# A decoder layer on one NeuronCore: the plan of attention's last quarter drawn up anew, with 42 identity transposes added on TensorE

## What is computed

```
x = x + self_attention(layernorm(x))            # 16 heads of 64, causal
x = x + cross_attention(layernorm(x), ctx, mask) # one head of 256, 64 context rows a batch
x = x + ffn(layernorm(x))
ffn(h): h = silu(h @ w1 * s1) * (h @ w2 * s2)   # 256 -> 1024
        h = gelu(h @ h1 * s);  h = gelu(h @ h2 * s)   # 1024 -> 1024, twice
        return h @ w3 * s                        # 1024 -> 256
```

## Time and profile before

| | |
|---|---|
| median of three runs | 1535.09 us (1532.70, 1535.09, 1535.42) |
| the profiled execution | 1538.07 us, of which its span, first to last instruction, is 1536.3 us |
| busy of the span | PE 98%, PEld 83%, DVE 71%, ACT 62%, POOL 31% |
| mean granted TensorE clock | 0.992 of full speed |

### The profile page before, as it was taken

One profiled execution on the slowest core, in us unless ns is written; L12 is line 12 of the kernel. 1 busy time (PEld: TensorE's weight loads), 2 busy tenths in 40 slices (PEclk: granted clock), 3 DMA queues, 4 the chain that ended last, 5 costly groups with the idle time before them and its releaser, 6 DMA issues.

```text
span 1536.3 us, 29271 instructions
## 1 busy us (share of the span) xinstructions
PE 1506.7 (98%) x10784; PEld 1281.0 (83%) x10784; DVE 1092.3 (71%) x2748; ACT 956.1 (62%) x2246; POOL 482.7 (31%) x763
## 2 busy tenths in 40 slices
PE   8999999999999999999998899999999999999998
PEld 6888888888888888888887788888888888888887
DVE  7999999999999999998999456644553533433432
ACT  5988788888788888888887454445444532222222
POOL 2545454454544445545451001100110211111110
PEclk8999999999999999999999999999999999999999
DMA  4000000000000000000024223421112622222221
GB/s 151 2 1 2 29 2 29 1 2 29 1 29 1 2 29 2 29 1 2 22 90 138 106 79 115 131 103 69 62 70 101 208 88 84 84 83 83 83 84 42
DMA packets 55769, 87.16 MB, mean 57 GB/s; under 512 B 4160, under 2 KB 33216, under 8 KB 55616
## 3 DMA queue, kind: packets, MB, share of 16 engines
q1 hardware_dynamic: 55616, 85.10, 16.4%
HBM read 55.72 MB, written 29.36 MB: 55 GB/s over the span
## 4 chain that ended last, share of the span: by engine, by line
PE 89%; DVE 5%; ACT 2%; DMA 2%; issue 1%; POOL 0%; SPq 0%; DVEq 0%
PE bank L988 14%; PE bank L990 12%; PE bank L634 10%; PE bank L554 9%; PE bank L606 8%; PE bank L556 7%; PE bank L555 7%; PE bank L618 6%; PE bank L996 2%; PE bank L1096 2%; PE bank L1088 2%; PE bank L1089 2%; PE bank L1090 2%; DMA pf<-h_scratch 1%; PE bank L1118 1%; PE bank L1127 1%
## 5 line engine op out<-in xcount | busy, mean ns | idle before, releaser
L820 POOL TENSOR_SCALAR P<-P,stats 128x512 f32<-128x512 f32 (+3 forms) x512 | 267.8, 542 | 362.8 <-DVE stats L798 362.7
L693 ACT ACTIVATE P<-P,stats 128x128 f32<-128x128 f32 (+3 forms) x512 | 283.7, 560 | 19.0 <-DVE stats L790 18.6
L657 ACT ACTIVATE PT<-bank 128x512 fp32r<-128x512 f32 (+1 forms) x384 | 185.7, 524 | 85.2 <-PE bank L618 84.3
L790 DVE CUSTOM_DVE_ANT_0 P<-bank,cmask 128x512 f32<-128x512 f32 (+3 forms) x512 | 228.9, 483 | 3.2 <-PE bank L606 2.4
L707 DVE TENSOR_TENSOR PT<-bank,PT 128x512 fp32r<-128x512 f32 (+1 forms) x384 | 218.6, 594 | 4.9 <-ACT PT L657 3.5
L1267 DVE TENSOR_TENSOR Hb<-gt,Hb 128x512 fp32r<-128x512 f32 x128 | 90.7, 710 | 162.8 <-ACT Hb L1135 162.0
L988 PE MATMUL bank<-w,hw 128*128 128x512 f32 x512 | 200.9, 392 | 4.2 <-DVE w L1267 4.2
L988 PE MATMUL bank<-Hb,hw 128*128 128x512 f32 x512 | 203.1, 397 | 0.0
L634 PEld LDWEIGHTS bank<-PT,V 128*128 128x128 f32 x1024 | 164.3, 189 | 17.1 <-DVE PT L707 0.7
L990 PE MATMUL bank<-Hb,hw 128*128 128x512 f32 x448 | 175.4, 391 | 0.0
L634 PE MATMUL bank<-PT,V 128*128 128x512 f32 (+3 forms) x1024 | 174.7, 318 | 0.0
(11 more groups left out here) (218 smaller groups left out, 3327.2 us busy)
## 6 DMA issues: line engine op xcount, KB each, us to landing
h_scratch<-go SPq DMA_DIRECT2D x64, 256.0 KB, 2.1
xs<-x_scratch SPq DMA_DIRECT2D x23, 512.0 KB, 4.0
qf<-h_scratch SPq DMA_DIRECT2D x32, 256.0 KB, 4.0
pf<-h_scratch SPq DMA_DIRECT2D x32, 256.0 KB, 4.9
stageA<-in_h SPq DMA_DIRECT2D x14, 512.0 KB, 3.8
x_scratch<-x SPq DMA_DIRECT2D x8, 512.0 KB, 3.1
x_scratch<-xs SPq DMA_DIRECT2D x8, 512.0 KB, 3.0
out<-xns SPq DMA_DIRECT2D x16, 256.0 KB, 2.3
```

The source lines that it names most:

```text
L657: return e.activation(dst, src, ACT.Copy, scale=scale)
L693: e.activation(p, p, ACT.Exp, bias=st_[:, k:k + 1], scale=-1.0, accum_out=st_[:, 8 + k:9 + k]).then_inc(s_exp, 1)
L790: e.tensor_tensor_reduce(P_tile(P, i, a), banks["S", P, max(i, 1)][a][:, slice(*S_COLS[i])], cmask[:, 512 - n:512], -1.0, 3.0e38, ALU.add, ...
L820: e.tensor_scalar(p, p, stats[P % 4][:, k:k + 1], 1.0, ALU.mult, ALU.mult).then_inc(s_norm, 1)
```

## The change

The four tables of `TAIL` are replaced (SP's too, by one move). Each engine has the same steps as before, in another order; `HEAD`, `BATCH` and `later()` are untouched. In addition a helper gives TensorE 20 transposes of the identity matrix ahead of `AV.63.0`, and 22 ahead of `xt.0.1.0`, all of them written into the bank that the step has just claimed and then overwrites.

```diff
     "SP": """
-        xload.0 st.6 mb ld.0 ld.1 ld.2 ld.3 ld.6 ld.5 ld.4 ld.7 ld.8 ld.9 ld.10 ld.11 ld.13 st.7 ld.14 ld.12
+        xload.0 st.6 mb ld.0 ld.1 ld.2 ld.3 ld.6 ld.5 ld.4 ld.7 ld.8 ld.9 ld.10 ld.11 ld.13 ld.14 st.7 ld.12
         ld.15 xload.1 ld.16""",
...
+    def keep_warm(e, out, n):
+
+
+        for _ in range(n):
+            e.transpose(out[:, 0:128], ident[:, :], ident[:, :])
+
...
             out, = claim(w, ("AV", P, a))
+            if (P, a) == (NP - 1, 0):
+                keep_warm(e, out, 20)
             w.wait_ge(s_vlo, 4 * (P // 4) + 4)
...
                 out, = claim(w, item)
+                if a == [0, 1, 0]:
+                    keep_warm(e, out, 22)
                 w.wait_ge(s_ln2, ln_at(b, which) + 4)
```

More of the change, by code:

```diff
@@ L115 @@
     "PE": """
[L116 to L125, removed]
@@ L126 @@
-    "ACT": """
[L127 to L148, removed]
@@ L149 @@
-    "DVE": """
[L150 to L174, removed]
@@ L175 @@
[L175 to L185 removed]
+        S.54.2 k.55 v.57 T.53.1 O.52 q.55 S.54.1 T.53.0 k.56 S.55.3 S.55.2 AV.53.0 T.54.2 AV.53.1 T.54.0 S.55.1
@@ new lines @@
+        T.54.1 q.56 k.57 AV.54.0 AV.54.1 O.53 S.56.3 T.55.1 O.54 S.56.2 T.55.2 S.56.1 T.55.0 v.58 v.59 q.57
+        AV.55.0 AV.55.1 S.57.3 T.56.2 T.56.0 v.60 S.57.2 S.57.1 T.56.1 k.58 q.58 AV.56.0 AV.56.1 O.55 T.57.2
+        S.58.3 S.58.2 S.58.1 T.57.0 v.61 T.57.1 k.59 AV.57.0 q.59 AV.57.1 O.56 T.58.2 S.59.3 T.58.0 S.59.2
+        S.59.1 v.62 v.63 k.60 T.58.1 AV.58.0 q.60 AV.58.1 O.57 T.59.2 S.60.3 T.59.0 S.60.2 S.60.1 k.61 T.59.1
+        q.61 AV.59.0 O.58 S.61.3 T.60.2 S.61.2 S.61.1 AV.59.1 k.62 T.60.0 T.60.1 q.62 xt.0.0.0 AV.60.0 AV.60.1
@@ new lines @@
+    "DVE": """
+        ql.54 ys.52.0 lsum.0.0 ys.52.1 vl.56 pl.53.2.0 os.51 r.53.0 m.54.3.0 pl.53.2.1 m.54.2.0 m.54.2.1
+        m.54.3.1 kl.55 lnorm.0.0 pl.53.1.1 os.52 r.54.2 vl.57 pl.53.1.0 m.54.0.1 m.54.1.0 ql.55 m.54.0.0
+        m.54.1.1 pl.53.0.1 pl.53.0.0 kl.56 m.55.2.1 r.54.0 m.55.3.1 m.55.3.0 m.55.2.0 ys.53.0 pl.54.2.0
+        pl.54.2.1 pl.54.0.0 m.55.1.1 m.55.0.0 ys.53.1 m.55.0.1 pl.54.0.1 pl.54.1.0 pl.54.1.1 m.55.1.0 r.55.2
+        ql.56 kl.57 r.55.0 ys.54.0 ys.54.1 os.53 m.56.3.1 m.56.3.0 pl.55.1.0 os.54 pl.55.1.1 m.56.2.0 pl.55.2.1
+        m.56.0.0 m.56.0.1 pl.55.2.0 m.56.2.1 pl.55.0.0 m.56.1.0 pl.55.0.1 r.56.2 m.56.1.1 vl.58 vl.59 ql.57
+        r.56.0 ys.55.0 ys.55.1 m.57.3.0 pl.56.2.0 m.57.3.1 pl.56.0.0 pl.56.2.1 pl.56.0.1 vl.60 m.57.1.1 m.57.0.0
+        m.57.0.1 pl.56.1.0 m.57.2.0 m.57.2.1 pl.56.1.1 m.57.1.0 r.57.2 r.57.0 kl.58 ql.58 ys.56.0 ys.56.1 os.55
+        pl.57.2.1 pl.57.2.0 m.58.3.0 m.58.2.1 m.58.2.0 m.58.0.0 m.58.0.1 m.58.3.1 pl.57.0.1 m.58.1.0 pl.57.0.0
+        m.58.1.1 pl.57.1.1 vl.61 pl.57.1.0 r.58.2 ys.57.0 kl.59 ql.59 r.58.0 ys.57.1 os.56 pl.58.2.1 pl.58.2.0
+        m.59.3.0 m.59.3.1 m.59.2.1 m.59.1.0 m.59.0.1 m.59.0.0 m.59.2.0 pl.58.0.0 pl.58.0.1 vl.62 m.59.1.1 bqa
+        vl.63 kl.60 pl.58.1.1 pl.58.1.0 r.59.2 r.59.0 mask ys.58.0 ql.60 ys.58.1 os.57 pl.59.2.1 pl.59.2.0
+        m.60.3.0 m.60.3.1 pl.59.0.0 m.60.2.0 pl.59.0.1 m.60.1.0 m.60.2.1 m.60.1.1 m.60.0.0 m.60.0.1 kl.61 r.60.2
+        pl.59.1.1 ql.61 pl.59.1.0 r.60.0 os.58 ys.59.0 m.61.3.0 m.61.2.0 m.61.2.1 m.61.1.1 m.61.1.0 m.61.3.1
+        m.61.0.1 m.61.0.0 pl.60.2.1 pl.60.2.0 ys.59.1 kl.62 pl.60.0.1 pl.60.0.0 pl.60.1.0 pl.60.1.1 r.61.2
+        xtl.0.0.0 ql.62 ys.60.0 r.61.0 ys.60.1 xtl.0.0.1 os.59 pl.61.2.1 pl.61.2.0 m.62.3.0 m.62.2.1 m.62.3.1
+        m.62.2.0 fl.0 pl.61.0.0 m.62.0.0 os.60 fl.1 pl.61.1.1 m.62.1.0 pl.61.0.1 kl.63 r.62.2 m.62.1.1 fl.2
+        ql.63 m.62.0.1 ys.61.0 fl.3 xka.0 pl.61.1.0 bql xkl.0 r.62.0 xka.1 fl.4 ys.61.1 xkl.1 pl.62.2.0 m.63.2.0
+        m.63.2.1 m.63.3.1 pl.62.2.1 xva.0 xva.1 m.63.3.0 xfl.0 fl.5 r.63.2 xfl.1 m.63.1.0 pl.62.1.0 m.63.1.1
+        pl.62.0.0 pl.62.1.1 m.63.0.0 pl.62.0.1 m.63.0.1 fl.6 xvl.0 r.63.0 xs1.0 xs2.0 xs3.0 xs4.0 os.61 ys.62.0
+        xvl.1 xr.0 ys.62.1 pl.63.0.0 pl.63.2.1 xpl.0 pl.63.0.1 pl.63.1.0 pl.63.1.1 xoa.0.0 os.62 fl.7 pl.63.2.0
+        xoa.0.1 lsum.0.1 ys.63.0 fl.8 xva.2 ys.63.1 lnorm.0.1 xva.3 flag.2 fl.9 xtl.0.1.0 xtl.0.1.1 fl.10 fm.2
+        fl.11 xvl.2 xvl.3 os.63 os.64 hm.0.0 hm.0.1 hl.0.0 hm.0.2 hl.0.1 hm.0.3 hl.0.2 hl.0.3 hm.0.4 fl.12
+        hl.0.4 hm.0.5 lsum.1.0 flag.3 hl.0.5 fm.3 hm.0.6 hm.0.7 lnorm.1.0 hl.0.6 hl.0.7 fl.13 fl.14 fl.15 fl.16
+        flag.0""",
```

40 lines of the change are left out of this document (36 added, 4 removed).

## The result

The changed kernel takes 1538.18 us (median of 8 runs, 1536.06 to 1541.4), the kernel before 1534.95 us (8 runs). The ratio is 1.0023, 95% interval 1.0014 to 1.0033: 2.2 to 5.1 us slower, by the best value 3.5. The medians themselves are 3.2 us apart.

A forecast was written before the change was run, and what follows sets the result against it. It took TensorE to bound attention from 672 to 788 us and VectorE's queue the end, 788 to 823; 0.45 + 0.7 + 0.0 to 0.1, about +1.1 us, on the median 1535.09 gave 1536.2 us, range 1531.0 to 1539.5.

The forecast's parts named there:

- case A: Whole kernel: the forecast itself, with both new costs, at the 20 transposes and at `xs.1`; 1534 to 1538 us, chance 0.50.
- rival C: Both batches: transposes don't raise the clock, so the 20 take 4.4 us and `ys.63.0` is 4.5 late; 1539.0 us, chance 0.16.
- part 1: Order up to `lnorm.0.1`: VectorE's 2.9 us idle goes, 1.0 us of small operations comes; its end moves from 822.35 to 820.4.
- L: End of `lnorm.0.1`, 822.35 us in the kernel before; forecast 822.8, 0.45 us later.
- part 2: 20 transposes ahead of `AV.63.0`: behind the claim, they begin where the wait ends; `ys.63.0` 1.6 to 3.3 us late, 2.4 taken.
- part 3: 22 transposes ahead of `xt.0.1.0`: they run in TensorE's wait for `lnorm.0.1`, 2.4 us at high clock in 3.5 left; no cost.
- part 4: From `lnorm.0.1`'s end to `xs.1`: a 4.0 us wait replaces the 4.46; resumes 1.2 us earlier, net 0.7 later with low clock.
- part 5: 672 to 788 us: slack at `AV.53.0` turns from 1.6 to -0.4 us; between 0 and 1.6 lost, 0.1 taken.
- I take 1.9: Low clock behind the wait at `xs.1`: 1.9 us lost, from 2.1 and 1.7 lost behind two earlier waits.
- D: 672 to 788 us: up to 1.6 us lost on TensorE, none absorbed, besides the likeliest case's costs; 1537.7 us, chance 0.14.
- B's mild form: The 20 cost VectorE nothing and `fl.12` isn't held up, low clock stays: gain 3.55, 1531.5 us; chance 0.20 with both forms.
- B's form without the low clock: Same gains at the 20 and `fl.12`, and no low clock behind the wait at `xs.1`: 1529.6 us, chance 0.05.

The follow-up runs named there:

- e5: Changed kernel with `xs.1` of the first batch behind `h.0.2`, both batches of transposes where the change puts them: 1531.28 us, ratio 0.9979 to the kernel before.
- e4: Changed kernel with 34 more identity transposes behind the claim of `xs.1`'s bank, ahead of the wait for its input: 1534.03 us, ratio 0.9994 to the kernel before.
- e12: Changed kernel without both batches of transposes and with the first batch's `xs.1` behind `h.0.2`: 1530.78 us, ratio 0.9974 to the kernel before.
- e1: Changed kernel with both batches of transposes taken out, only the new order left: 1538.10 us, ratio 1.0019 to the kernel before.
- e2: Changed kernel without the 20 transposes ahead of `AV.63.0`, the 22 kept: 1536.07 us, ratio 1.0011 to the kernel before.
- e3: Changed kernel with the 20 transposes put ahead of `AV.63.0`'s claim, in the free bank `xv.2` takes later: 1534.37 us, ratio 0.9996 to the kernel before.
- e10: Changed kernel with the 20 transposes in a free bank ahead of the claim and 34 more ahead of `xs.1`: 1532.77 us, ratio 0.9989 to the kernel before.
- e11: Changed kernel with the 20 in a free bank, plus 12 matmuls of 512 columns ahead of `xs.1`'s 24 of 64: 1537.93 us, run once, no ratio.
- e7: Changed kernel with the 20 in a free bank ahead of the claim and the first batch's `xs.1` behind `h.0.2`: 1528.70 us, ratio 0.9960 to the kernel before.

## Why the prediction came out so

It said 1536.2 us and within 0.2%, range 1531.0 to 1539.5; it is 1538.18, in the range, by the mechanisms of its likeliest case A and at the upper end of "same". A's own range ended at 1538; that the result lies well inside the whole range is owed to rival C, for whose sake the range went up to 1539.5 and whose mechanism didn't occur. That much is luck. The sign and the places were right, the size was not: +1.1 forecast, +3.2 by the medians and +4.0 by the traces. Step by step, the measured side from `q.54`:

| term | forecast | measured |
|---|---|---|
| part 1, order up to L | -1.95 | -2.19 (order alone) |
| part 2, the 20 transposes | +2.4 | +3.37 |
| part 3, the 22 | 0 | 0, wait of 1.46 left |
| part 4, `xs.1` from L | -1.2 | -1.57 (L + 34.12, before L + 35.69) |
| part 4, low clock behind the wait | +1.9 | +4.43 |
| part 5, 672 to 788 | 0 to +0.1 | in part 1 |
| sum | about +1.1 | +4.04 |

**Part 1** held: without the 3.12 us of wait of `ys.63.0`, L of after would be 820.29 - 3.12 = 817.17, or 820.4 with the 3.25 us of the head: the forecast number.

**Part 2** had the mechanism: the claim comes first, so the batch begins where the wait ends. Its two ends were 1.6 us late at the high clock and 3.3 at the low one, and both were seen: 1.8 (L 153.58 in e5, against 151.80) and 3.4 (L 155.15 and 155.17 in after and e4). I took the middle of two cases that don't mix within one execution. The 0.22 us for a transpose at the low clock came from a row over which the profile shows a clock of 1.00; e4's 20, which began at 0.50 and ran so for 2.8 us, took 3.77 us in all, which fits 0.22. In six executions with about 2.75 us idle there, the clock fell in three (after, e4, e12) and not in the others (e1, e2, e5).

**Part 3** held, also the length: 22 in 2.57 us.

**Part 4**, the wait: forecast as 4.0 us, released by `XTs`, at L + 34.5, with four `big` in a row on ScalarE before it and none at `xt.1.0`. It is 3.95 us, `XTs`, L + 34.1, four `big`. The step from the end of the last split to that of `xtl.1.0`, 5.0 us in the earlier trace rows, is 5.0 again: 852.97 + 1.29 less 848.06 + 1.21.

**The step that failed** is "I take 1.9" for the clock behind that wait. I took it from two waits of before, with 3.4 and 4.2 us at 0.50 behind them. The low clock behind the wait at `xs.1` lasted 10.2 us and cost 4.4 us by the table above, 4.8 by the kernel that fills the wait. With 1.9 replaced by 4.4 to 4.8 the sum is 3.6 to 4.0.

Two things were wrong in it. The first is in the trace of before: the 4.2 us are only the end of a low stretch that began at 848.9, while TensorE still waited.

```profile
848.90:851.40 2.50, 0.00 (x0) 0.00 (x0) 2.50 (x7) 2.40 (x5) 0.92 (x1) 0.50 0.01 3
```

So the whole stretch had 6.8 us, of which 2.6 fell into the idle time and cost nothing. At `xs.1` the clock fell within 0.5 us of the wait's end in all four kernels with this wait and nothing added, so nearly the whole stretch hit work; in e3 it had 6.8 us too, and cost 3.2 us (`xs.1` to `g.1.0` took 30.74 us, and 27.54 in e10, where the clock stayed up). The second is that it lasted 10.2 us in the other three. Behind the waits of before stand matmuls of 256 and 512 columns and eight transposes of 128; behind the wait at `xs.1` stand 24 of 64 columns. That these lengthen the stretch is what e11 suggests, in one execution.

**Part 5** was right in its sum, but its sign was a bad one. TensorE's idle from 672 to 788 us is 116 - 114.76 = 1.24 us, "above 1 us", which I had named as the mark of D. It cost nothing at L: the order alone gives the L that part 1 forecast with all of this idle in it. `AV.53.0`, where I expected it, has no wait. VectorE, which sets the end there, didn't see it.

**The rivals.** B's mild form (the 20 cost VectorE nothing) is what e3 makes true, and it gives no 1531.5, since the low clock is dearer. B's form without the low clock, 1529.6, is near e7. C is refuted by the rows: 20 in 2.34 us (e3), 22 in 2.57 (after) and 34 in 3.87 us (e4), all at 1.00. The rule of the Trainium skill (page "TensorE: Matmul & The Clock Gate", section "Part 4: PE-mode transpose"), by which transposes don't count as work for the clock, is not what this chip did: with 34 of them in the wait of `xs.1` the clock stayed at 1.00 in two kernels of two, without them it fell in five of five. By C I would have got 1539.0, near the result, for a wrong reason.

## What to carry to other kernels

Work that is meant to fill a wait has to stand ahead of everything that can wait, the claim of its bank too; behind it, it delays the very step that was waited for. Price a wait of TensorE by the low clock behind it as well as by its length, and by when the clock falls: here 3.9 us of idle were followed by 3.2 to 4.8 us lost at the low clock. Best is to put real work in the wait: moving one step by one place gained 5.5 us here (e3 to e7, by their ratios), over twice what all the transposes brought (2.1).

## What the runs showed of the hardware

- The clock behind a wait. About 4 us of idle ahead of 24 matmuls of 64 columns: at 0.50 for 10.2, 10.2, 10.2 and 6.8 us. The same idle ahead of 12 matmuls of 512 columns: 3.4 us, in one execution. In the kernel before, 4.46 us of idle ahead of transposes and then matmuls of 512 columns: 6.8 us, the first 2.6 of them idle.
- The level is not fixed by the program: the same 2.75 us of idle, same instructions up to there, was followed by 0.50 in e12 and by 1.00 in e1. And e5 had 3.4 us at 0.50 behind a wait of 0.34 us, which e7 and e12, with waits of 0.34 and 0.36, had not. The fall needn't come at the wait's end: it came 0.4 us ahead of it in e12, 1.3 us behind it in the changed kernel (809.8 against 808.47) and 2.1 us behind it in e5. What decides stays open.
- `lnorm.0.1` took 2.83 us and `lnorm.1.0` 1.37, for the same four 128x256 operations (VectorE's rows above). Beside the first GpSimd ran two operations on `Y` (below), beside the second none. Whether they slow it down was not tested.

```profile
817.52 0.62 POOL L834 TENSOR_SCALAR Y<-Yf 128x512 fp32r<-128x512 f32 x1 [5.15 <-DVE Yf L776]
818.22 1.27 POOL L839 TENSOR_TENSOR Y<-Yf,Y 128x512 fp32r<-128x512 f32 x1
```
